# A two-stage image kernel on one core: copies, a logarithm, statistics, a load and row copies moved to other units

## What is computed

```
x = x + L0(gn(x))
    key     = softmax over pixels of (Kw . q + Kb)            49 x 1024, q = gn(x)
    filters = relu(norm(conv0 . (q . key)))                   256 x 49
    L0      = depthwise 7x7 convolution of q with (conv1 . filters)
x = x + L1(gn(x))
    x', z   = split(in_w . gn(x));   f1, f2, f3 = three levels (32x32, 16x16, 8x8) of x'
    y_l     = ssm(f_l) + flip(ssm(flip(f_l))) + upsampled y_(l+1)
    ssm:      delta = softplus(...), h_t = h_(t-1) * exp(delta_t A) + delta_t B_t x_t,
              y_t = sum over 16 states of h_t * C_t, then a norm over channels
    L1      = out_w . (y_1 * silu(z))
```

## Time and profile before

| | us |
|---|---|
| three runs: lowest, median, highest | 3894.95, 3897.47, 3903.98 |
| the profiled execution: its time, and its span | 3897.22, 3895.4 |
| busy: PE, DVE, ACT, POOL | 3129.9, 3016.8, 2696.6, 3086.7 |
| mean granted clock of PE | 0.896 |

### The profile page before, as it was taken

One profiled execution on the slowest core, in us unless ns is written; L12 is line 12 of the kernel. 1 busy time (PEld: TensorE's weight loads), 2 busy tenths in 40 slices (PEclk: granted clock), 3 DMA queues, 4 the chain that ended last, 5 costly groups with the idle time before them and its releaser, 6 DMA issues.

```text
span 3895.4 us, 54301 instructions
## 1 busy us (share of the span) xinstructions
PE 3129.9 (80%) x13644; PEld 1584.7 (41%) x13644; DVE 3016.8 (77%) x3847; ACT 2696.6 (69%) x6662; POOL 3086.7 (79%) x1588
## 2 busy tenths in 40 slices
PE   6988887987878898788888878898787879878632
PEld 3544344443434444344444434444443444443210
DVE  1058788787888878788887888788788887888887
ACT  4467676767777687776768767676776767676542
POOL 0049789796978979798796978879697897969797
PEclk8999898998898999899999989899898989989765
DMA  1026455564555546454564645455464555636454
GB/s 45 1 99 212 165 181 184 181 206 140 202 168 180 200 156 207 155 193 163 186 212 142 210 147 196 168 193 204 139 213 160 185 179 180 208 132 215 166 197 166
DMA packets 187326, 665.46 MB, mean 171 GB/s; under 512 B 22736, under 2 KB 24672, under 8 KB 186976
## 3 DMA queue, kind: packets, MB, share of 16 engines
q1 hardware_dynamic: 186976, 661.47, 50.0%
HBM read 639.76 MB, written 21.63 MB: 170 GB/s over the span
## 4 chain that ended last, share of the span: by engine, by line
PE 21%; POOL 21%; issue 20%; ACT 16%; DVE 12%; DMA 8%; DVEq 1%; POOLq 1%; SPq 0%; ACTq 0%
PE pconv L842 12%; POOL bx L1466 11%; DMA bb<-bc_rows 8%; POOL y L1501 7%; ACT diag L1161 5%; DVE h L607 4%; DVE slot_c L598 3%; PE pm L851 2%; PE pm L923 2%; ACT slot_b L1283 2%; PE pm L869 1%; ACT a L1274 1%; POOL h L1496 1%; POOL delta L1436 1%; ACT es L1236 1%
## 5 line engine op out<-in xcount | busy, mean ns | idle before, releaser
L842 PE MATMUL pconv<-pad,diag 128*128 128x464 f16 (+11 forms) x9408 | 2083.3, 376 | 166.8 <-DVE xn L520 99.8
L842 PEld LDWEIGHTS pconv<-pad,diag 128*128 128x128 f16 x9408 | 919.7, 99 | 1312.9 <-issue 288.4
L1501 POOL TENSOR_TENSOR y<-y,h 128x1024 f32<-128x1024 f32 (+1 forms) x544 | 1229.4, 2260 | 153.0 <-DVE h L607 149.2
L1283 ACT ACTIVATE slot_b<-delta,nega 128x512 f32<-128x512 f32 (+1 forms) x1280 | 809.6, 641 | 746.2 <-DVE slot_c L598 608.4
L1466 POOL TENSOR_TENSOR bx<-bb,u 128x1024 f32<-128x1024 f32 x512 | 1220.4, 2385 | 9.7 <-DMA bb<-bc_rows 9.0
L598 DVE TENSOR_TENSOR_SCAN slot_c<-slot_b,bx 128x512 f32<-128x512 f32 (+1 forms) x768 | 783.9, 1043 | 225.1 <-POOL bx L1466 144.8
L607 DVE TENSOR_TENSOR h<-slot_c,cb 128x512 f32<-128x512 f32 x1152 | 773.2, 672 | 0.0
L598 DVE TENSOR_TENSOR_SCAN slot_c<-slot_b,slot_c,bx 128x512 f32<-128x512 f32 x512 | 663.2, 1295 | 67.4 <-ACT slot_b L1283 9.6
L1161 ACT ACTIVATE diag<-id,chi 128x128 f16<-128x128 f16 x1568 | 496.1, 387 | 9.0 <-PE pconv L842 9.0
L1161 ACT ACTIVATE diag<-id,clo 128x128 f16<-128x128 f16 x1568 | 496.1, 387 | 0.0
L923 PE MATMUL pm<-h,cen 128*128 128x256 f32 x1024 | 251.1, 389 | 12.9 <-POOL h L1478 6.5
(11 more groups left out here) (182 smaller groups left out, 3250.1 us busy)
## 6 DMA issues: line engine op xcount, KB each, us to landing
bb<-bc_rows SPq DMA_DIRECT2D x592, 512.0 KB, 4.6
cb<-bc_rows SPq DMA_DIRECT2D x592, 512.0 KB, 4.4
xr<-in_x SPq DMA_DIRECT2D x16, 1024.0 KB, 5.0
out<-ob SPq DMA_DIRECT2D x16, 1024.0 KB
bc_rows<-rows SPq DMA_DIRECT2D x64, 64.0 KB, 3.2
w<-in_w SPq DMA_DIRECT2D x2, 256.0 KB
wc<-in_wc SPq DMA_DIRECT2D x2, 256.0 KB
bc_rows<-rows SPq DMA_DIRECT2D x16, 32.0 KB, 4.5
```

Source lines behind the costliest of these rows:

```text
L842: ins = nc.tensor.matmul(img(bank(pconv, k), W)[:, r0:r1, c0:c1], w, pad[:, t, part, 16 * k + r0 + dy:16 * k + r1 + dy, c0 + dx:c1 + dx], ...
L1283: ins = nc.scalar.activation(slot_b[:, o:o + w], delta[:, so + c:so + c + w], ACT.Exp, scale=nega[:, st, n0 + n:n0 + n + 1])
L1501: pool.tensor_tensor(yv, yv, src[:, 0] if len(src.shape) == 3 else src, ALU.add).then_inc(q_y.sem, 1)
```

## The change

Nothing that is computed changes. On SP, `get_b(2)` and `get_c(2)` move from unit 0 to the bridge ahead of it, before the store of the output; the load of `xr` moves from unit 2 to unit 5. On DVE, the statistics of image m move from unit 3 to units 8 and 9, half each, and three steps of chunk 4 move by half a unit to a unit. On PE, one tap of the convolution (six matmuls, L842) moves behind `lower(1)`, `chunk_bc(0)` and `chunk_dt(0)`. On ACT, `keep_x` moves from unit 1 to 3, `copy_x` from unit 1 to 4, `a_xh_` from unit 12 to 14, `chunk_log` moves ahead of the diagonal passes of its unit (for chunk 4 to the start of unit 14), 7 diagonal passes move from unit 34 to 35, and 5 of them from the last unit to the bridge. On POOL, `inputs(6)` moves ahead of `weigh` of product 9, `f_affine` ahead of the gather of its unit, `chunk_low(4)` from unit 14 to 15.

```diff
 SP
-                    if k + 2 < NU:
+                    if 2 < k + 2 < NU:
                         get_b(i, k + 2)
                         get_c(i, k + 2)
...
-                if k == 2 and j is not None and m is not None:
+                if k == 5 and j is not None and m is not None:
                     sp.wait_ge(a_copy.sem, a_copy.at(m, 0))
                     sp.dma_start(xr[:, :, :], xv[m]).then_inc(x_in.sem, 16)
...
                     get_b(j, 1)
                     get_c(j, 1)
+                    get_b(j, 2)
+                    get_c(j, 2)
                 if i is not None:
                     sp.wait_ge(ob_ready.sem, ob_ready.at(i + 1, 0))
 DVE
-                stats(m, sa, xr, a_stats)
+                stats(sa, xr, (0,))
+
+            def a_s1(m):
+                stats(sa, xr, (1,)).then_inc(a_stats.sem, 1)
...
-            pre = {3: a_s0, 18: a_max_, 20: a_dg_, 21: a_ktc_, 22: a_fic_, 23: a_f2c_, 28: a_scale_}
+            pre = {8: a_s0, 9: a_s1, 18: a_max_, 20: a_dg_, 21: a_ktc_, 22: a_fic_, 23: a_f2c_, 28: a_scale_}
 PE
                         lower(j, 0)
-                    if m is not None:
-                        taps(m, BRIDGE_TAPS[1], BRIDGE_TAPS[2])
-                    if j is not None:
                         lower(j, 1)
                         chunk_bc(j, 0)
                         chunk_dt(j, 0)
+                    if m is not None:
+                        taps(m, BRIDGE_TAPS[1], BRIDGE_TAPS[2])
 ACT
                     copy_z(j)
                 if m is not None:
+                    make_row(m, 1, 9)
                     make_row(m, RING - 2, 0, KK)
...
-            pre = {10: a_mean_, 11: a_rstd_, 12: a_xh_, 17: a_keyb_, 18: lambda m: (a_xtc_(m, 0), a_xtc_(m, 1)),
+            pre = {10: a_mean_, 11: a_rstd_, 14: a_xh_, 17: a_keyb_, 18: lambda m: (a_xtc_(m, 0), a_xtc_(m, 1)),
...
-                if k == PREP + 1:
-                    if j is not None:
-                        b_normal(j)
+                if j is not None and k == PREP + 1:
+                    b_normal(j)
+                if k == PREP + 2:
                     if m is not None:
                         make_row(m, 0, KK)
-                if k == PREP + 2:
-                    if m is not None:
                         prep(m, 1)
...
                         copy_f(j, 2)
-                    if m is not None:
-                        make_row(m, 1, 9)
...
-                    if k == 1:
-                        chunk_log(i, 2)
+                    if k in (1, 14):
+                        chunk_log(i, {1: 2, 14: 4}[k])
...
                         decay(i, k + 1, 0)
+                    if k in CHUNK_LOG:
+                        chunk_log(i, CHUNK_LOG[k])
...
-                    if k in CHUNK_LOG:
-                        chunk_log(i, CHUNK_LOG[k])
...
-                    if k == 1:
+                    if k == 3:
                         keep_x(i)
-                if j is not None and k == 1:
+                if j is not None and k == 4:
                     copy_x(j)
 POOL
                 if i is not None:
+                    if k == 5:
+                        inputs(i, k + 1)
                     for q in products_of(k - 1):
                         if q in POOLED:
                             weigh(i, q)
-                    if k + 1 < NU:
+                    if k + 1 < NU and k != 5:
                         inputs(i, k + 1)
+                if m is not None and k == 26:
+                    f_affine(m)
+                if i is not None:
                     for v in (k - 1, k) if k == NU - 1 else (k - 1,):
 tables
-CHUNK_FIRST = {(1, -4): 2, (2, -1): 3, (13, -1): 4, (15, -1): 5}
-CHUNK_LOG = {2: 3, 13: 4, 15: 5}
-CHUNK_LAST = {(1, -1): 2, (3, -4): 3, (14, -2): 4, (16, -2): 5}
-CHUNK_LOW = {1: 2, 3: 3, 14: 4, 16: 5}
+CHUNK_FIRST = {(1, -4): 2, (2, -1): 3, (14, -2): 4, (15, -1): 5}
+CHUNK_LOG = {2: 3, 15: 5}
+CHUNK_LAST = {(1, -1): 2, (3, -4): 3, (15, -2): 4, (16, -2): 5}
+CHUNK_LOW = {1: 2, 3: 3, 15: 4, 16: 5}
```

More of the change, by code:

```diff
@@ L461, in _, with stats @@
             dve.wait_ge(setup, DVE_SET + ACT_SET)
-            def stats(b, s, x, done):
-                for t in range(CT):
+            def stats(s, x, ts):
+                for t in ts:
                     for k in range(2):
                         ins = nc.vector.bn_stats(s[:, 12 * t + 6 * k:12 * t + 6 * k + 6], bank(x[:, t, :], k))
-                ins.then_inc(done.sem, 1)
+                return ins
             def a_s0(m):
@@ L524, in b_s0 @@
                 dve.wait_ge(conv_out.sem, conv_out.at(i, CT))
-                stats(i, sg, xn, b_stats)
+                stats(sg, xn, (0, 1)).then_inc(b_stats.sem, 1)
             def chunk_first(i, c):
@@ L1528, in unit @@
                 if m is not None:
-                    if k == 26:
-                        f_affine(m)
                     if k == 28:
```

## The result

| | before | after |
|---|---|---|
| median (runs), us | 3902.30 (12) | 3882.23 (12) |
| ratio after to before | | 0.9949, 95% interval 0.9939 to 0.9959 |
| the profiled execution: its time, and its span | 3897.22, 3895.4 | 3877.74, 3875.9 |
| forecast, range | | 3842, 3812 to 3876 |

It is faster by 0.51%, some 20 us; the forecast was 55, and the measured time lies 6 us outside the range. The direction was right, the size was not.

What follows compares the result with a forecast made beforehand. Bound by POOL, so gains were read from its idle stretches. Terms of -3.1, -0.25 and -0.5 us gave -3.85 per body, -54 over 14 loop bodies, and -1 for body 14: 3897.2 - 55 = 3842 us, range 3812 to 3876.

Steps and rivals of the forecast that it cites:

- term B: Units 1 to 7: POOL's input 8, set by the load of bb, starts slightly sooner; -0.25 us per body, bounds -2.6 to +1.0.
- I take 6.6 us: Units 1 to 7: assumed landing time of bb queued behind xr and cb, so input 8 starts at about 1676.2.
- the third of the bodies that have no wait for this load: Input 8: in a third of bodies, without a wait for bb now, the change would cost +0.4 us.
- The estimate by the Trainium skill: Load of bb before input 8: 2.1 MB issued from 1668.7 in at about 1675.5, input 8's gain about -1.0 us.
- term A: Unit 14: POOL's 3.54 us wait for DVE goes, 0.4 us given back in unit 15; -3.1 us per body.
- term C: Filters' chain: f_affine one gather sooner removes POOL's waits for `w_low` in five loop bodies; -0.5 us per body.
- They are worth nothing: Bridge: early get_b(2), get_c(2) shrink POOL's 7.39 us idle before input 2, but the gather behind waits for ACT's `y_start`.
- late `y_start`: Bridge: moved diagonal passes on ACT and six matmuls on PE make `y_start` end 2.2 us later.
- It is no term of its own: Bridge: the 2.2 us lateness of `y_start` is covered by DVE's 4.00 us in units 1 to 7, so not counted separately.
- The statistics: Units 8 and 9: 2 x 1.22 us more on DVE fit its reserve; cost 0 to 0.8 us, taken as 0.
- Rival 2: Input 8: bb lands late behind xr, costing +1.0 us per body there; 3860 us, chance 0.18.
- Rival 5: Gains only uncover another wait: PE's `flat_add` chain or late `y_start` delays unit 5 equally; 3895 us, chance 0.07.

Runs made afterwards that it cites:

- e8_getb2_alone: The kernel before with one edit only: get_b(2) and get_c(2) go out in the bridge ahead of the store of the output; 3892 us, ratio 0.9954.

## Why the prediction was wrong

The forecast was 35 us too good, and the stretches say where: 14 x 1.25 = 17 us in units 1 to 7 with the bridge, 12 us in the filters' chain, 6 us in unit 14. Another 5 us of the distance to 3842 come from its base, 3897.2 us from one execution, where the twelve runs have 3902 in the median.

**Units 1 to 7, term B, the step that failed most.** "I take 6.6 us" for bb behind xr: it took 8.5. I had priced it by the load behind xr in unit 2, where the queue had 0.5 MB less in front, and added 0.8 us for that. The rest of the chain came as worked out: silu's product at 1661.2 (1661.4), product 9 done at 1668.2 (1668.5), `get_b(8)` out at 1669.3 (1669.6), all in the time of before. Input 8 started at 1677.9 and not at 1676.2, and term B is +1.1 us in this body, +1.0 in the mean, just the bound that the prediction gives to the late load. A smaller slip: "the third of the bodies that have no wait for this load" are two or three of 14. The estimate by the Trainium skill (DMA: Bandwidth & Descriptors, anatomy of one DMA), 1675.5, lies further off from the measured 1677.9 than mine; it prices transfers of GpSimd's kind, and these are SyncE's, queued behind each other.

**Unit 14, term A.** Right in mechanism: the wait of 3.54 us is gone. Mis-sized: 2.65 us by the stretch, about 2 us by the runs, not 3.1. The "0.4 us" that is given back is 0.84. And with chunk 4 undone in the changed kernel the wait is 2.80 us, not 3.54. POOL starts input 8 some 0.8 us later there than in the kernel before and may have that much less to wait for; this was not tested.

**The filters' chain, term C.** Wrong: f_affine had time to spare, and TensorE's backlog of taps sets `whi`. I had seen the wait but not what the matmul behind it waited for. The stretch got 0.4 us longer where 0.5 less was forecast: nine of 13 bodies have the wait, where six had it before.

**The bridge.** "They are worth nothing" was read from POOL's timeline: input 2 was idle time in front of another wait. That is true, and POOL was the wrong engine to ask. TensorE's pause at the loop's turn grows with the two loads, by 2 us a body in the changed kernel. The body that I read has one of the short pauses, 3.34 us; over 13 bodies it went from 3.1 to 5.9 us, and this was in the profile to be seen. For the late `y_start` 2.2 us were forecast and 1.8 measured. "It is no term of its own" holds against the kernel before, since product 9 ended when the working said. But undoing the edits brings product 9 and input 8 forward by 1.0 us, so the lateness eats a gain that the change would otherwise have. Neither error explains the missing 35 us. They hid each other: without the early loads the time would have been 3912 us, without the bridge's edits 3868.

**The statistics.** Right: no wait of POOL's for DVE in units 8 to 13 of the changed kernel.

**The rivals.** Rival 2, the late load, was right in mechanism and in price. It gave 3860 because it kept terms A and C; with what these two measured, another 18 us, it comes to 3878, and the profiled execution took 3877.74. Rival 5 named the flat_add chain and the late `y_start`, and gave 3895; both were at work. None had the pause at the turn.

**What the parts are worth** in the changed kernel, by undoing or moving one: loads early 28 us, chunk 4 27 us, f_affine nothing; the bridge costs 15 us, and xr ahead of get_b(8) and not behind get_c(8) 42 us. They need not add up, since each wait can stand in for another. The copies and chunk 3's logarithm, the statistics and input 6 were never undone, so what they bring is not shown.

## What to carry to other kernels

A load that is moved is to be priced for the loads behind it in the queue too, by a row with as many bytes in front of it, and here the one of 1 MB belonged behind the load that is waited for, not ahead of it. Two traces are to be lined up on an event that the change can't have moved; here input 0 had moved, and input 36 of the body ahead had not. In a loop, look at what DMA traffic runs at the loop's turn, and at the engines' pauses there, body by body: a pause that varies is a cost that can be moved. When a wait ends in a matmul, ask what the matmul itself stood behind.

## What the runs showed of the hardware that was not expected

- TensorE's pause at the loop's turn is 2.8 to 3.1 us with less DMA traffic (43 to 55% of the DMA engines' time in the 12 us around it, in the changed kernel and in e8_getb2_alone), and 3.1 to 7.3 us in the four kernels with 1 MB of loads more at that time. In 14 executions of kernels that have the loads ahead of the store, 180 of 182 pauses are between 2.7 and 3.4 us, the other two 3.7 and 4.0.
- A load of 512 KB with 0.5 MB and 1 MB issued 1.1 and 0.5 us ahead of it lands in 8.5 us, with 2 MB issued in the 2.1 us ahead of it in 9.5, and with 0.5 MB 0.4 us ahead of it in 4.8. The 1 MB itself takes 6.4 us in the first case.
- Bodies of one loop that run the same instructions differ by 3 us in the kernel before. One half goes with the pause at the turn, in four of five long bodies. The other is a wait of 1.4 us; in the changed kernel it goes with a stretch at the lower clock 30 to 40 us before, behind a wait for dg in the body looked at. What tips it was not settled.
